# Attention of a two-layer block: where the pairs of row-maximum matmuls stand among the scores

## The reference

```python
x = x + attention_a(layernorm(x))   # 16 query heads, 4 key/value heads, head size 16, biases, rotary embedding
x = x + ffn(layernorm(x))           # 256 -> 2048 -> 256, gated GELU, weights from packed 4-bit codes
x = x + attention_b(layernorm(x))   # 16 query and 16 key/value heads, head size 16
x = x + ffn(layernorm(x))           # the same ffn weights
```

## Time and profile before

| what | value |
|---|---|
| median of 3 runs | 1843.65 us (1842.32, 1843.65, 1855.19) |
| profiled execution, its own time | 1850.14 us |
| its span, first to last instruction | 1848.3 us |
| mean granted TensorE clock in it | 0.965 |
| PE busy / LDWEIGHTS busy | 93% / 59% |
| DVE (VectorE) busy | 62% |
| ACT (ScalarE) busy | 51% |

### The profile page before, as it was taken

How to read it: one execution, slowest core, us unless ns; L and a number is a source line. 1 busy time by engine, 2 the same in 40 slices (tenths; PEclk the granted TensorE clock), 3 DMA queues, 4 the chain that set the end, 5 groups by cost and what they waited for, 6 DMA issues and landing times. The chain is left out here.

```text
span 1848.3 us, 32629 instructions
## 1 busy us (share of the span) xinstructions
PE 1721.0 (93%) x13230; PEld 1096.3 (59%) x13230; DVE 1145.4 (62%) x1664; ACT 951.0 (51%) x1883; POOL 544.4 (29%) x454
## 2 busy tenths in 40 slices
PE   6789899999999989999978988899999998999998
PEld 5444444554445568888866533445544455788887
DVE  6457767677876366554574477676777653754554
ACT  2234556666777634444422345667667774344443
POOL 5213547587687412333320010000000000233332
PEclk9788998999999999999997899999999999999999
DMA  5114106115011060000003141060240002400000
GB/s 142 39 31 61 38 28 106 35 55 90 23 44 74 36 273 1 1 1 1 0 20 126 61 60 33 4 90 2 30 64 1 36 2 85 190 12 1 12 11 12
DMA packets 50483, 89.24 MB, mean 48 GB/s; under 512 B 20920, under 2 KB 35000, under 8 KB 48072
## 3 DMA queue, kind: packets, MB, share of 16 engines
q1 hardware_dynamic: 45560, 70.99, 16.4%
q0 software_dynamic: 4256, 15.78, 2.7%
q10 hardware_dynamic: 528, 0.52, 0.1%
HBM read 58.17 MB, written 28.84 MB: 47 GB/s over the span
## 5 line engine op out<-in xcount | busy, mean ns | idle before, releaser
L1166 DVE TENSOR_REDUCE chunk_max<-ring 128x2 f32<-128x1024 f32 (+3 forms) x640 | 668.5, 1063 | 273.5 <-PE ring L898 177.4
L1061 ACT ACTIVATE probs<-ps_s 128x512 f32<-128x512 f32 (+3 forms) x1280 | 619.6, 534 | 359.2 <-PE ps_s L924 177.5
L1469 POOL TENSOR_TENSOR inter_lo<-inter,inter_hi 128x512 fp32r<-128x512 f32 x128 | 165.6, 1294 | 904.8 <-ACT inter_hi L1417 904.8
L898 PE MATMUL ring<-xnt 63*128 63x512 f32 (+3 forms) x640 | 231.3, 463 | 29.8 <-DVE chunk_max L1166 11.7
L898 PE MATMUL ring<-region_rounded 63*128 63x512 f32 (+3 forms) x640 | 247.4, 441 | 11.5 <-DVE chunk_max L1166 10.3
L924 PE MATMUL ps_s<-xnt 64*128 64x512 f32 (+3 forms) x640 | 239.5, 432 | 7.4 <-ACT probs L1061 6.0
L924 PE MATMUL ps_s<-region_rounded 64*128 64x512 f32 (+3 forms) x640 | 230.4, 443 | 5.0 <-ACT probs L1061 5.0
L924 PEld LDWEIGHTS ps_s<-xnt 64*128 64x128 f32 x640 | 108.5, 190 | 148.4 <-ACT probs L1061 108.3
L1398 ACT ACTIVATE gelu_a<-ps_g 128x512 f32<-128x512 f32 x128 | 76.5, 598 | 218.3 <-PE ps_u L87 218.3
L1442 DVE SCALAR_TENSOR_TENSOR gelu_a<-gelu_a,ps_g 128x512 f32<-128x512 f32 x128 | 88.0, 687 | 156.0 <-ACT gelu_a L1398 155.7
L943 PE MATMUL ps_o<-probs,region_plain 128*32 128x256 f32 (+1 forms) x2304 | 179.2, 383 | 0.0
(11 more groups left out here) (203 smaller groups left out, 2879.5 us busy)
## 6 DMA issues: line engine op xcount, KB each, us to landing
w_mlp<-w_scr SPq DMA_DIRECT2D x32, 768.0 KB, 15.7
w_scr<-region_rounded POOLq DMA_DIRECT2D x16, 768.0 KB, 3.8
region_rounded<-q_scr SPq DMA_DIRECT2D x24, 256.0 KB, 8.2
q_scr<-region_rounded SPq DMA_DIRECT2D x16, 192.0 KB, 2.4
xnt<-q_scr SPq DMA_DIRECT2D x12, 256.0 KB, 8.9
xnt<-w_scr SPq DMA_DIRECT2D x4, 768.0 KB, 5.5
q_scr<-region_rounded SPq DMA_DIRECT2D x8, 384.0 KB, 3.6
k_scr<-region_rounded SPq DMA_DIRECT2D x8, 384.0 KB, 3.7
```

The costliest lines, as they stand in the source:

```text
L898: op = pe.matmul(out[:, h, 0:w], qt[g][plain[h], p, q0:q0 + P], kt[g][plain[h], p % NKP, c * TW:c * TW + w], start=True, stop=c < t)
L1061: act.activation(pr[n % NPR][:, h, w0:TW], src[:, 0:TW - w0], ACT.Exp, scale=SCALE).then_inc(s_e, 1)
L1166: dve.tensor_reduce(mp[rank[y[1:3]] % 2][:, qb, 2 * p:2 * p + 2, c], ring[n % 2][:, :, 0:w], AX.X, ALU.max).then_inc(s_rd, 1)
L1469: pool.tensor_tensor(il[n % NI][:, :], ti[n % 2][:, :], ih[n % NI][:, :].bitcast(F32), ALU.subtract).then_inc(s_il, 1)
```

## The change

A pair may only begin behind an even score (head 0 or 2). A pair that is open is closed behind the next score, as before.

```diff
                 plan.append(("S", g, t, kb, h))
-                if made < ahead(s) or made % 2:
+                if h % 2 == 0 and made < ahead(s) or made % 2:
                     x = pairs[made // 2]
                     plan.append(x + (1 - h % 2,))
                     made += 1
```

## The result

The changed kernel takes 1759.06 us (median of 4 runs, 1756.36 to 1762.40) against 1844.62 us (median of 4, 1842.32 to 1855.19): ratio 0.9526, 95% interval 0.9484 to 0.9569. The profiled executions are 1761.64 and 1850.14 us, 88.5 us apart. I had forecast 1775, by a sum of 69 us: right in sign and in the mechanism of the wait, short by some 16 us.

A forecast was written before the change was run, and what follows sets the result against it. Ring-slot waits, from pairs held open across a PV, were taken to bound the kernel, not PE or VectorE. Gains of 36 us in attention b and 33 in a, together 69, took 1843.65 to about 1775 us; range 1752 to 1816.

The forecast's parts named there:

- What bounds it: Large tiles: waits for a ring slot held across a PV stretch half-steps to mean 1.42 us; PE needs 1.24.
- the order's arithmetic: Large tiles: the slot comes free 0.2 us late before; after, reduction ends at 2.13, next pair at 2.48, 0.35 spare.
- Large tiles of groups 1 and 2: Groups 1 and 2, per attention: waits vanish and half-steps last 1.24 us; 17 us counted, bounds 0 and 20.
- Tile (0, 3): Group 0: a step falls from 3.28 to 2.61 us on 15 of 16 steps; gain 10 us, bounds 0 and 12.
- Group 3: Last group: some half-steps without any pair last 1.00 us against 1.24; 2 us counted, up to 3.8.
- the sum for group 0: Group 0 of attention b: the gains of its four tiles, 10 + 5 + 2 = 17 us.
- (0, 2): Group 0 tile with 8 pairs on 3 steps: 5 us counted, bounds -3 and 7.6.
- (0, 0) and (0, 1): Group 0 tiles with projections and mostly whole pairs: 2 us gain, between -2 and 5.
- That group 0 would not gain: Rival: reductions and whole pairs in a row bound group 0, only groups 1 to 3 gain, 1806 us; chance 0.15.
- That the ring is too short: Rival: two ring slots are too few, so the waits only move to another score, 1844 us; chance 0.06.
- The slower one: Rival: the wait stands before the second score of a half-step, holding it back 0.34 us each, 1909 us; chance 0.05.

The follow-up runs named there:

- The probe: The changed kernel with a short second VectorE reduction, read from PSUM, added ahead of each of the 640 reductions: 1814.89 us, ratio 0.9799 to the kernel before.
- the fastest variant: The changed kernel without group 0's fillers ahead of whole pairs and with group 0's PV cut in two: 1747.60 us, ratio 0.9452 to the kernel before.

## Why the prediction was right, and where it was short

*What bounds it* and *the order's arithmetic* held. The slot being 0.2 us late because a PV lay in the open pair was the cause: two kernels that exchange the PV's place exchange 41.6 and 46.5 us.

*Large tiles of groups 1 and 2.* (2, 3) forecast at 41.6, measured 41.55; (1, 3) 42.0 and 43.43. The two groups together gained 8.3 + 9.0 = 17.4 us in attention b, against 17. That this agrees so well is luck: a stall eats some (see the last section), and the clock fell from 1.00 to 0.98 and 0.97 there. In the experiment with the new rule in groups 1 to 3 only, where the clock stayed at 1.00, they gained 21.9.

*Tile (0, 3).* Forecast 2.61 us a step and a gain of 10; measured 2.61 and 9.3.

*Group 3.* Forecast 2, measured 2.3 in attention b, with the 1.00 us half-steps that were forecast.

*The step that was mis-sized* is the sum for group 0: 10 + 5 + 2 = 17 us, where attention b shows 26.85. Tile (0, 3), where the clock was 1.00 before and after, gave 9.3 of it; (0, 2) gave 8.7 where I counted 5, and (0, 0) and (0, 1) gave 8.8 where I counted 2. I treated the granted clock of 0.93 as a reason to count less, never as a term. It was one: PE stood still in front of the ring in group 0, and the clock there fell to its lower level of 1.2 GHz several times; with the waits shorter, and the fillers in place, it stays at 1.00. The wait of the earlier trace rows, 0.88 us up to 1114.01, and one of 0.40 us behind it are followed by this stretch of the kernel before:

```profile
1115.30:1118.70 3.40, 3.40 (x16) 1.29 (x16) 1.60 (x3) 0.60 (x1) 0.00 (x0) 0.50 0.77 192
```

A mean clock of 0.93 over the 176.85 us of group 0 is 2 x 0.07 x 176.85 = 25 us at half speed. The price comes from the kernel before against itself: its fastest run, 1838.78 us, had clock 0.973, its slowest, 1858.98, had 0.957; that is 20.2 us for 2 x 0.016 x 1848 = 59 us at half speed, 0.34 each. So, as an estimate, 25 x 0.34 = 8.4 of the 26.85 are the clock's, and 18.4 are left against my 17.

Over the whole execution the clock explains less than that suggests, because groups 1 and 2 of attention b went the other way. The mean clock was 0.965 over 1848.3 us and is 0.972 over 1759.8: 2 x (0.035 x 1848.3 - 0.028 x 1759.8) = 31 us fewer at half speed, 10.5 us by this price. The profiled executions are 88.5 us apart where I had 69, so I was short by 19.5 us: about half of it is the clock's, and some 9 us are the terms of the order. By the same estimate 4 of these lie in groups 1 and 2 of attention b (17.4 gained, and 3.8 lost to the clock, against 17), 1.4 in group 0 there, and most of the rest in attention a. The 0.34 is a relation between whole executions, not a shown cause: a run with more waiting could also be the one with the lower clock. Single tiles of one and the same kernel agree with it roughly: tile (3, 0) of attention b took 10.06 us at clock 1.00 in one profile of the kernel after and 11.48 at 0.85 in the other, 0.42 us for each us at half speed. No run changes the clock of group 0 and nothing else.

*The rivals.* That group 0 would not gain fell: it gained most. That the ring is too short, by the rule on consistent bubbles, which stands in the Trainium skill, "Perfetto Trace Analysis", under Optimization Strategy, fell too: the same two slots serve at 1.24 us. The slower one did not come about. The probe shows which stretch is nearest to it: about 0.1 us more per full reduction costs 0.8 us in the large tile (2, 3) and 14 us in group 0.

## What to carry to other kernels

A buffer that is filled by two instructions is held from the first to the last, so what stands between them in an in-order queue counts as its hold time; put the long foreign instruction between two fillings, not inside one. When half-steps alternate between two lengths though no engine needs their mean, write down the times at which a slot is taken, filled and freed against one period: the late one shows at once. Where a stall is removed from a stretch in which the granted clock was below 1.00, price the clock too, from runs of the same kernel at different clocks, and over the whole execution: other stretches can lose what this one gains.

## What the runs showed that I had not expected

A stall for which the profile names no releaser. In attention b, tile (2, 2) began with 3.67 us in which the weight loads waited, and the clock was 0.50 from 1276.10 to 1282.90, right behind it:

```profile
1275.95 0.19 PEld L898 LDWEIGHTS ring<-xnt 63*128 63x128 f32 x2 [3.67 <-issue]
```

The DMAs that load the next group's heads run at that time. Besides them the profile shows a packet of instructions: in the 4.5 us from 1272.0 on, one of 16 KB on queue 8, which starts at 1272.5, 0.3 us into the stall, and takes 1.84 us:

```profile
q8 instruction: 1, 0.02, 2.6%
```

Nine of the profiles have a stall of 2.3 us or more in tile (2, 1) or (2, 2) of attention b, and in all nine such a packet of about 1.84 us starts within 1.2 us of the stall's begin. But other packets as long pass without a stall, one in tile (2, 1) of the fastest variant among them. That the weight loads wait for instructions is an idea that fits, and isn't shown. Tile (2, 2) took 36.9 us before, 37.2 and 36.9 in the two profiles of the kernel after, 34.0 with the new rule in groups 1 to 3 only, and 31.6 in the fastest variant, with the same order in that tile and no long stall. Up to 5.6 us of attention b so depend on something that the change only moved: the stall, and the half clock behind it.
